# The complement of the mask bytes: from VectorE in the last stage to ScalarE in the second stage

## What is computed

```
layer 0: w = masked_row_softmax(adj^T);  region = batch_norm(w h k1 + b1)
         people = batch_norm(w^T region k2 + b2);  x = x + people
layer 1 (A): attention, scores leaky_relu(s_i + t_j), entries with adj == 0 excluded
layer 2 (B): e = einsum('bid,bjd,dk->bkij', h, h, A); with adj in {0, 1} only
         scores = where(adj == 1, leaky_relu(e_0), NEG); x = x + softmax(scores) h
layer 3 (C): as layer 1, then elu
```

## Time and profile before

| | |
|---|---|
| median of three runs | 1788.75 us |
| the profiled execution | 1788.1 us |
| its span | 1786.3 us |
| TensorE matmul busy | 1495.2 us (84%) |
| VectorE busy | 1336.9 us (75%) |
| ScalarE busy | 1187.9 us (66%) |
| mean granted clock of TensorE | 0.953 |

### The profile page before, as it was taken

How to read it: one execution, slowest core, us unless ns; L and a number is a source line. 1 busy time by engine, 2 the same in 40 slices (tenths; PEclk the granted TensorE clock), 3 DMA queues, 4 the chain that set the end, 5 groups by cost and what they waited for, 6 DMA issues and landing times. The chain is left out here.

```text
span 1786.3 us, 33876 instructions
## 1 busy us (share of the span) xinstructions
PE 1495.2 (84%) x12740; PEld 1198.0 (67%) x12740; DVE 1336.9 (75%) x3885; ACT 1187.9 (66%) x1841; POOL 187.2 (10%) x201
## 2 busy tenths in 40 slices
PE   3999996997459698898888989898888889888863
PEld 3999995554337386776767667586776768667653
DVE  3666655886456788888888888888888888887763
ACT  2777871222355877777787877878777787876751
POOL 3344410000000010000001000010000001000000
PEclk9999996999569899999999999999999999999986
DMA  9999942777111020302203032120303203021010
GB/s 186 214 212 210 212 105 84 247 249 258 48 33 63 25 77 19 107 16 92 83 25 95 19 101 61 47 84 25 102 12 100 84 24 95 19 66 50 11 44 29
DMA packets 108456, 162.03 MB, mean 91 GB/s; under 512 B 9344, under 2 KB 59136, under 8 KB 106240
## 3 DMA queue, kind: packets, MB, share of 16 engines
q1 hardware_dynamic: 85248, 117.86, 21.5%
q0 software_dynamic: 18432, 33.56, 10.2%
q10 hardware_dynamic: 4608, 8.39, 1.3%
HBM read 151.40 MB, written 41.94 MB: 108 GB/s over the span
## 5 line engine op out<-in xcount | busy, mean ns | idle before, releaser
L1265 PE MATMUL ps<-fac_C,mask_C 128*128 128x258 f16 x2048 | 241.8, 276 | 48.5 <-DVE xC L951 25.3
L1265 PE MATMUL ps<-fac_A,mask_A 128*128 128x258 f16 x2048 | 236.9, 274 | 25.0 <-DVE prod L895 13.3
L1265 PEld LDWEIGHTS ps<-fac_C,mask_C 128*128 128x128 fp8e4 x2048 | 198.3, 98 | 88.5 <-DVE xC L951 29.5
L1327 PE MATMUL ps<-hV,wts 128*128 128x129 f32 x2048 | 243.6, 274 | 2.7 <-DVE xC L951 1.2
L1265 PEld LDWEIGHTS ps<-fac_A,mask_A 128*128 128x128 fp8e4 x2048 | 198.9, 98 | 63.4 <-DVE prod L895 20.1
L1327 PEld LDWEIGHTS ps<-hV,wts 128*128 128x128 f32 x2048 | 236.1, 191 | 3.8 <-DVE prod L895 1.4
L939 DVE SCALAR_TENSOR_TENSOR wts<-lk,wts 128x1024 f32<-128x1024 f32 x128 | 155.3, 1221 | 46.0 <-ACT wts L1184 44.9
L1183 ACT ACTIVATE lk<-ps 128x1024 f32<-128x1024 f32 x128 | 131.7, 1029 | 73.2 <-PE ps L1318 47.2
L307 ACT ACTIVATE maskT<-ps 128x1024 fp8e4<-128x1024 bf16 x128 | 131.3, 1026 | 50.3 <-PE ps L341 38.6
L1162 ACT ACTIVATE mask_A<-s_row,steep_t_A 128x1024 fp8e4<-128x1024 f32 x128 | 143.1, 1138 | 1.8
L1184 ACT ACTIVATE wts<-ps,shiftB 128x1024 f32<-128x1024 f32 x128 | 143.2, 1119 | 0.0
(11 more groups left out here) (240 smaller groups left out, 3176.8 us busy)
## 6 DMA issues: line engine op xcount, KB each, us to landing
adj_b<-in_adj POOLq DMA_DIRECT2D x128, 256.0 KB, 9.2
maskT_scratch<-maskT SPq DMA_DIRECT2D x16, 1024.0 KB, 6.9
ring_A<-maskT_scratch SPq DMA_DIRECT2D x64, 256.0 KB, 3.1
off<-maskT_scratch SPq DMA_DIRECT2D x32, 512.0 KB, 6.5
ring_C<-maskT_scratch SPq DMA_DIRECT2D x64, 256.0 KB, 4.0
xa<-in_x SPq DMA_DIRECT2D x16, 512.0 KB, 4.3
whT_scratch<-whT_s ACTq DMA_DIRECT2D x32, 256.0 KB, 6.4
whT_b<-whT_scratch SPq DMA_DIRECT2D x16, 512.0 KB, 4.8
```

The source lines that it names most:

```text
L1265: last = nc.tensor.matmul(Q_SLOTS[c % 2][:, k, 0:XW], m_fp8[x][:, k, j, c * P:c * P + P], fac[x][:, k, j, :], start=(j == 0), stop=(j == T ...
L1327: last = nc.tensor.matmul(Q_SLOTS[c // 2 % 2][:, c % 2, 0:PW], wts[:, j, c * P:c * P + P], hV[b % 2][:, j, :], start=(j == 0), stop=(j == ...
```

## The change

In the second stage ScalarE makes the complement of each graph's mask bytes by two activations with `Identity`, scale -1 and bias 2056 = 8 * 257. Two bytes are read as one uint16 number, so that both bytes of it are complemented at once: each activation handles four row tiles, 128 x 2048 numbers. They stand behind `graph(b+2)` in the order of ScalarE and ahead of `people(b+1)`; for the last two graphs ahead of the `people` of the same graph. SyncE stores both halves to a new scratch tensor, in `save(b)` behind the store of `pT_b`, each behind a wait for its activation; the buffer has one place for each half. In the last stage `off` is loaded from the new scratch tensor; `complement` goes, and `gram` waits for the load.

```diff
+        offT_dram = nc.dram_tensor("offT_scratch", (B, P, T, N), u8).ap()
...
+            off_b = sbb("off_b", [P, 2, T // 2, N], u8)
+            two_edges = sbb("two_edges", [P, 1])
...
                     def save(b, par):
...
                         sp.dma_start(pTf_dram[bass.ds(b, 1)].rearrange("a p n -> (a p) n"), pT_b[:, par, :]).then_inc(b_pT_out[par], 16)
+                        for h in range(2):
+                            sp.wait_ge(b_off, 2 * b + h + 1)
+                            sp.dma_start(offT_dram[b, :, h * T // 2:(h + 1) * T // 2, :], off_b[:, h, :, :]).then_inc(b_off_out[h], 16)
...
+                    for h in range(2):
+                        sp.wait_ge(b_off_out[h], 16)
...
-                        sp.dma_start(off[:, 4 * h:4 * h + 4, :], maskT_dram[0, :, 4 * h:4 * h + 4, :]).then_inc(off_in[h], 16)
+                        sp.dma_start(off[:, 4 * h:4 * h + 4, :], offT_dram[0, :, 4 * h:4 * h + 4, :]).then_inc(off_in[h], 16)
...
+                        sp.wait_ge(b_off_out[par], B * 16)
...
+                    nc.vector.memset(two_edges[:, :], float(EDGE * 257)).then_inc(b_two, 1)
...
+                    def no_edges(b):
+                        for h in range(2):
+                            if b > 0:
+                                act.wait_ge(b_off_out[h], b * 16)
+                            nc.scalar.activation(off_b[:, h, :, :].bitcast(u16), maskT[:, b, h * T // 2:(h + 1) * T // 2, :].bitcast(u16),
+                                                 ACT.Identity, bias=two_edges[:, 0:1], scale=-1.0).then_inc(b_off, 1)
...
                     graph(0, 0, 0, True)
                     graph(1, 1, 0, True)
+                    act.wait_ge(b_two, 1)
+                    no_edges(0)
                     people(0, 0, 0, True)
                     graph(2, 0, 1, False)
                     people(1, 1, 0, True)
                     graph(3, 1, 1, False)
+                    no_edges(1)
                     for k in range(1, B // 2 - 1):
                         for par in range(2):
                             people(k * 2 + par, par, k, False)
                             graph(k * 2 + 2 + par, par, k + 1, False)
-                    for par in range(2):
-                        people(B - 2 + par, par, B // 2 - 1, False)
+                            no_edges(k * 2 + par)
+                    no_edges(B - 2)
+                    people(B - 2, 0, B // 2 - 1, False)
+                    no_edges(B - 1)
+                    people(B - 1, 1, B // 2 - 1, False)
...
-                    def complement(b, h):
-                        dve.wait_ge(S["B", "ring"][h], (b + 1) * 16)
-                        nc.vector.tensor_scalar(off_int[:, 4 * h:4 * h + 4, :], off_int[:, 4 * h:4 * h + 4, :], EDGES, None,
-                                                ALU.bitwise_xor).then_inc(S["B", "off"], 1)
...
-                        if AA:
-                            complement(i, 0)
-                            complement(i, 1)
...
                         if j % 4 == 0:
-                            pe.wait_ge(S["B", "off"], 2 * b + j // 4 + 1)
+                            pe.wait_ge(S["B", "ring"][j // 4], (b + 1) * 16)
```

More of the change, by code:

```diff
@@ L11, in gnn_stack_kernel @@
     fp32, i32 = mybir.dt.float32, mybir.dt.int32
-    fp16, bf16, u8 = mybir.dt.float16, mybir.dt.bfloat16, mybir.dt.uint8
+    fp16, bf16, u8, u16 = mybir.dt.float16, mybir.dt.bfloat16, mybir.dt.uint8, mybir.dt.uint16
     fp8 = mybir.dt.float8e4
-    EDGE, EDGE_VALUE, EDGES = 8, 2.0 ** -6, 0x08080808
+    EDGE, EDGE_VALUE = 8, 2.0 ** -6
     ALU = mybir.AluOpType
@@ L536, in gnn_stack_kernel @@
             pT_b = sbb("pT_b", [P, 2, N])
+            off_b = sbb("off_b", [P, 2, T // 2, N], u8)
+            two_edges = sbb("two_edges", [P, 1])
+            b_off, b_off_out = stage_sem("b_off"), [stage_sem(f"b_off_out{k}") for k in range(2)]
+            b_two = stage_sem("b_two")
             b_mask_out = [stage_sem(f"b_mask_out{k}") for k in range(2)]
@@ L713, in gnn_stack_kernel @@
             ring_int = {x: ring[x][:, :, :].bitcast(i32) for x in cases}
-            off_int, off_fp8 = off[:, :, :].bitcast(i32), off[:, :, :].bitcast(fp8)
+            off_fp8 = off[:, :, :].bitcast(fp8)
             lk = sbc("lk", [P, 2, N])
@@ L752, in gnn_stack_kernel @@
                 S["C", n] = csem(f"C_{n}")
-            for n in ("var", "rstd", "shift", "h", "hT_made", "ahi", "lo", "off", "gram", "exps", "wts", "tile", "done"):
+            for n in ("var", "rstd", "shift", "h", "hT_made", "ahi", "lo", "gram", "exps", "wts", "tile", "done"):
                 S["B", n] = csem(f"B_{n}")
@@ L789, in load_off @@
                             sp.wait_ge(S["B", "gram"], (b - 1) * T + 4 * h + 4)
-                        sp.dma_start(off[:, 4 * h:4 * h + 4, :], maskT_dram[b, :, 4 * h:4 * h + 4, :]).then_inc(S["B", "ring"][h], 16)
+                        sp.dma_start(off[:, 4 * h:4 * h + 4, :], offT_dram[b, :, 4 * h:4 * h + 4, :]).then_inc(S["B", "ring"][h], 16)
                     def load_q(b):
```

## The result

The changed kernel takes 1912.1 us against 1788.6 us, a ratio of 1.069 (95% interval 1.068 to 1.071). It is 124 us slower; forecast were 126.

What follows compares the result with a forecast made beforehand. TensorE was taken to bound the second stage now, and a loop over SyncE's queue after the change. The last stage starting 141 us later, less 15 gained there, made +126 on 1788.1: 1914 us, likely 1875 to 1940.

Steps and rivals of the forecast that it cites:

- What bounds the second stage: Second stage before the change: TensorE sets the 8.69 us period; ScalarE idles 6.41 us between `people` and the next `row_hi`.
- The price of the pair: ScalarE, second stage: two added activations a graph, 2.0 us each, 3.9 us the pair (ends 3.6 and 4.3).
- The chain over SyncE: Second stage: load(b+3) queued behind stores awaiting b's pair closes a loop of 18.75 us a graph in place of 8.69.
- reaction and issue: SyncE, second stage: two queue reactions from the pair's end to the next load, 0.03 + 0.37 = 0.40 us.
- the landing with its handover: Second stage: load(b+3) lands in 4.8 us (4.2 to 5.8); handovers add 0.1 us.
- VectorE and the start of `row_hi`: Second stage: VectorE from L582 to the end of L594, 4.82 us, then ScalarE's `row_hi` starts; 4.91 us together.
- `row_hi` until the pair begins: ScalarE, second stage: 1.04 us of the chain; `row_hi` with its start was put at 1.13 us.
- The clock: TensorE, second stage: the clock falls in idle time, so rows take 3.6 us, not 1.95; full clock saves 20 us.
- The end: End of second stage: last pairs wait for stores, the final one behind first loads; last stage begins at 587.5, 141 us later.
- The last stage: Last stage: removing VectorE's complement gains 15 us (ends 0 and 22), from ScalarE's 1.13 us wait in 13 steps.
- The load does not bind: Rival, second stage: only the chain over `people` holds, 12.5 us a graph, 1839 us; chance 0.08.
- The pair runs in the idle time: Rival, second stage: the pair fits ScalarE's 6.41 us idle time, period stays 8.69 us, 1773 to 1782 us; chance 0.03.

Runs made afterwards that it cites:

- filler: Changed kernel with 32 matmuls whose result nobody reads, on TensorE between product(b) and rows(b+2): 1891.1 us, ratio 1.058.
- the removal alone: Kernel before without `complement`, nothing put in its place, `gram` waiting for the load: 1771.6 us, ratio 0.9906.
- the run that makes it so: Changed kernel with SyncE issuing the load of graph b+3 ahead of the stores of graph b's complement: 1833.8 us, ratio 1.025.
- pairs ahead: Changed kernel with the pair of graph b+2 behind `people(b)`, pairs 0 and 1 at the start, loads ahead of the complement's stores: 1776.7 us, ratio 0.994.
- the two GpSimd kernels: Kernel before with the last stage's complement on GpSimd: 1790.7 us, ratio 1.001; the same with GpSimd first waiting for VectorE's `averages(3)`: 1771.0 us, ratio 0.9896.

## Why the prediction was right

- *What bounds the second stage.* Right. The 8.69 us were TensorE's, with ScalarE's 6.41 us of idle time in the wrong place for the pair.
- *The price of the pair.* 3.9 us forecast, 3.89 measured.
- *The chain over SyncE.* Right, and shown: moving the load in SyncE's order alone takes 78 us away. The terms, forecast and measured: reaction and issue 0.40, 0.39; the landing with its handover 4.9, 4.69; the rows 3.6, 3.82; VectorE and the start of `row_hi` 4.91, 4.93; `row_hi` until the pair begins 1.04, 0.96; the pair 3.9, 3.89; sum 18.75, 18.68.
- *The clock.* Right, and shown with filler: 12 x 1.65 = 20 us forecast, 21 measured.
- *The end.* The last stage began at 591.3 for 587.5. Of this 2.5 us are the first stage, which was longer in this execution. The waits of the last two pairs were 2.6 and 12.3 us; I had 1.0 for the first and 11.3 for the second. But the reason given for the second was only half of it: the store stood behind the first loads, yet with the loads later ScalarE's wait went and the end of the stage stayed, then for the mask's last store. What bounds this end stays open.
- *The last stage.* The step was right (1.13 us for 1.15), and 15 us stand against 16.8 (13 to 21) for the removal alone.
- *The rivals.* "The load does not bind" is 1839 us, and the run that makes it so took 1834. "The pair runs in the idle time" took 1791 for 1773 to 1782, because its own late load closes another chain that I had not looked for; with the loads ahead of the stores as well it took 1777.

That the sum is right to 2 us is partly luck: in the profiled pair of executions the second stage cost 142.4 us for 141, the first stage, which has no part in it, 2.5 more, and the last stage gave back 21.1 for 15, of which 4.4 us were the three slow steps of the kernel before.

## What to carry to other kernels

Idle time of an engine only helps work that stands inside it in program order: behind the instruction that ends the idle time, 3.9 us cost 3.6 a graph at once. A wait put into a queue of transfers costs what stands behind it: here a load that had been issued 7 us early, and its landing time, a TensorE at its lower clock and VectorE's work closed a loop of 18.7 us. So for a wait added to a queue, write out the loop it closes, over every engine, and look for an order that puts loads ahead of stores.

## What was not expected of the hardware

- With the DMA engines busy for 0.96 of the time at 364 GB/s (pairs ahead, 340 to 420 us), TensorE and VectorE did not wait for them, and the loop's loads landed in 5.7 us (median) in place of 4.8.
- A GpSimd instruction of 1.9 us beside VectorE's copies of 8 numbers a partition made them take up to 1.48 us for 0.17: they ended with it. The traces of the two GpSimd kernels hold some other VectorE instructions beside GpSimd's. `TENSOR_SCALAR` of 8 numbers a partition from SBUF to SBUF ended with it too (`steep_t_A` took 1.49 us for 0.16, `te` 1.70 for 0.23, `rs_C` 1.41 for 0.17). Gathers and multiplications that read PSUM, statistics, and a reciprocal of two numbers from SBUF to SBUF (0.17 us) kept their times. What makes the difference was not tried.
- The first stage, which no kernel here touches, ended at different times: the first `row_hi` lay between 297.5 and 304.0 us over eleven profiled executions. The last stage agreed within 2.2 us in the nine traces that show its gain (1317.8 to 1320.0). So the first stage may be the largest part of the spread of a kernel's times (the kernel before: 1784 to 1794 us over all chips), but with one trace a kernel this isn't shown, and its cause stays open.
